# The scan's exponentiated rows: computed by ScalarE from rows already loaded, in place of stored once and loaded per chunk

## What is computed

```
a = -exp(log_a); dt = softplus(x @ Wdt.T + b_dt)
b, c = x @ Wb.T, x @ Wc.T                   # per head, state 64
state = exp(dt_t * a) * state + (dt_t * b_t) x_t      # step by step in time
y_t   = c_t . state
```

## Time and profile before

| | us |
|---|---|
| median of 3 runs | 1229.94 (1228.64 to 1230.48) |
| the profiled execution, its own time | 1230.54 |
| its span in the trace | 1228.7 |
| PE busy | 1208.2 (98%) |
| DVE, POOL, ACT busy | 949.7, 796.4, 611.8 |
| ecum_row loads | 128 of 128 KB, 3.7 to landing |

### The profile page before, as it was taken

One profiled execution on the slowest core, in us unless ns is written; L12 is line 12 of the kernel. 1 busy time (PEld: TensorE's weight loads), 2 busy tenths in 40 slices (PEclk: granted clock), 3 DMA queues, 4 the chain that ended last, 5 costly groups with the idle time before them and its releaser, 6 DMA issues.

```text
span 1228.7 us, 31470 instructions
## 1 busy us (share of the span) xinstructions
PE 1208.2 (98%) x12207; PEld 1012.2 (82%) x12207; DVE 949.7 (77%) x2028; ACT 611.8 (50%) x1279; POOL 796.4 (65%) x790
## 2 busy tenths in 40 slices
PE   8999999999999999999999999999999999999998
PEld 4666678888888888888888788898999889899998
DVE  7999977889876777777778667987777765776676
ACT  6999984434444443354344335543333332555454
POOL 4889955555555676776776648476666655576664
PEclk9999999999999999999999999999999999999999
DMA  9799756554455445555455456565544446799994
GB/s 298 261 337 356 288 214 170 149 157 146 157 157 160 154 146 170 161 150 164 149 148 168 126 171 212 190 156 91 109 91 90 97 87 125 251 320 322 336 332 166
DMA packets 140404, 231.40 MB, mean 188 GB/s; under 512 B 24416, under 2 KB 83040, under 8 KB 135648
## 3 DMA queue, kind: packets, MB, share of 16 engines
q1 hardware_dynamic: 127104, 212.10, 52.6%
q0 software_dynamic: 12288, 17.05, 8.1%
q10 hardware_dynamic: 864, 0.24, 0.1%
HBM read 147.81 MB, written 81.53 MB: 187 GB/s over the span
## 4 chain that ended last, share of the span: by engine, by line
PE 85%; DVE 5%; ACT 3%; DMA 3%; issue 2%; SPq 1%; POOL 1%; ACTq 0%; POOLq 0%; DVEq 0%
PE ps L1446 27%; PE ps L1808 11%; PE ps L2067 9%; PE ps L2301 7%; PE ps L2280 7%; PE ps L1527 4%; PE ps L1494 3%; PE ps L1553 3%; PE ps L1516 3%; PE ps L1538 2%; PE ps L1567 2%; PE ps L695 1%; DMA x_dram<-x 1%; PE ps L1787 1%; ACT tap L503 1%
## 5 line engine op out<-in xcount | busy, mean ns | idle before, releaser
L1408 ACT ACTIVATE decay<-tap,ncum 128x128 f32<-128x128 f32 x344 | 105.5, 389 | 191.7 <-POOL tap L1315 191.7
L1993 POOL DMA_INDIRECT ffn_dram<-ob,idx x64 | 110.5, 1727 | 81.8 <-DVE ob L1912 67.8
L2029 ACT ACTIVATE mid<-ps,b_up 128x512 f32<-128x512 f32 x96 | 66.1, 689 | 152.9 <-PE ps L1808 149.6
L1322 POOL TENSOR_TENSOR x_lo<-x,x_hi 128x512 fp32r<-128x512 f32 x56 | 76.9, 1372 | 100.4 <-ACT x_hi L1392 98.6
L1179 DVE TENSOR_TENSOR x_dt<-ps,dt 128x512 f32<-128x512 f32 x64 | 44.2, 691 | 126.4 <-PE ps L1553 126.3
L1446 PE MATMUL ps<-x_hi,w_hi_b 128*128 128x512 f32 x240 | 100.0, 416 | 2.0 <-issue 1.9
L1446 PE MATMUL ps<-x_hi,w_hi_c 128*128 128x512 f32 x240 | 99.3, 414 | 0.0
L2156 POOL TENSOR_SCALAR yc<-yc,gn_scale,gn_shift 128x512 f32<-128x512 f32 x56 | 76.3, 1374 | 33.1 <-DMA yc<-y_dram 33.1
L1446 PE MATMUL ps<-x_lo,w_hi_b 128*128 128x512 f32 x240 | 95.1, 396 | 0.0
L1408 ACT ACTIVATE decay<-cum_row,ncum 128x128 f32<-128x128 f32 x168 | 51.5, 391 | 86.8 <-POOL cum_row L1315 86.8
L1446 PE MATMUL ps<-x_lo,w_hi_c 128*128 128x512 f32 x240 | 94.2, 392 | 0.0
(11 more groups left out here) (321 smaller groups left out, 3996.9 us busy)
## 6 DMA issues: line engine op xcount, KB each, us to landing
tap<-cum_dram SPq DMA_DIRECT2D x86, 256.0 KB, 3.6
x_dram<-x SPq DMA_DIRECT2D x16, 1024.0 KB, 5.8
ecum_row<-ecum_dram SPq DMA_DIRECT2D x128, 128.0 KB, 3.7
yc<-y_dram SPq DMA_DIRECT2D x16, 1024.0 KB, 6.7
y_dram<-yb SPq DMA_DIRECT2D x60, 256.0 KB, 2.9
x<-x_dram SPq DMA_DIRECT2D x52, 256.0 KB, 3.9
cum_row<-cum_dram SPq DMA_DIRECT2D x42, 256.0 KB, 3.4
rows_dram<-xn SPq DMA_DIRECT2D x16, 512.0 KB, 3.3
```

The lines of the kernel that those rows point to most:

```text
L1322: nc.gpsimd.tensor_tensor(low, raw, high, ALU.subtract).then_inc(x_lo_ready, 1)
L1408: n = nc.scalar.activation(decay[g % 2][:, h, :], cum_row[g % NR][:, row, :], ACT.Exp, bias=t.ncum[:, g, h:h + 1])
L1993: pool.indirect_dma_start(out=t.ffn_dram, out_offset=bass.IndirectOffsetOnAxis(ap=t.idx[:, e, h * HC + c:h * HC + c + 1], axis=0), in_=ob[ ...
```

## The change

The exponentiated rows no longer go through DRAM. In the front, ecum, its transposes, its copy and its store are gone. In the scan ScalarE computes them from the rows of cum that are loaded anyway: exp_rows(g) waits for the load of those rows and for the product that last read its buffer, and writes ecum_row with two exponentials of 64 partitions x 512. In ScalarE's order exp_rows(g + 2) stands between b_part and c_part of chunk g (exp_rows(1) right after the first b_part). Since the mask overwrites the rows in place, causal(g) now waits for exp_rows(g) (ecum_ready). Chunks 0 and 32, which start with no state, have neither exp_rows nor c_dec. SyncE's 128 load_ecum are gone; the waits in front of the other transfers stay what they were, counted without the two chunks.

```diff
@@ front, VectorE
-            for i, bank in enumerate((ps_c, ps_dt)):
-                dve.wait_ge(ten, 3 + i)
-                do(v.tensor_copy(rowsT[:, i, :, :], bank[:, 0:GT * P].rearrange("p (g c) -> p g c", g=GT)),
-                   f"rows{i}")
+            dve.wait_ge(ten, 3)
+            do(v.tensor_copy(rowsT, ps_c[:, 0:GT * P].rearrange("p (g c) -> p g c", g=GT)), "rows")
@@ front, ScalarE
-            act.wait_ge(vec, steps["cum"])
-            nc.scalar.activation(tile_parity(ecum)[:, 0], by_tile_pair(t.cum[:, :, :])[:, 0], ACT.Exp)
-            nc.scalar.activation(tile_parity(ecum)[:, 1], by_tile_pair(t.cum[:, :, :])[:, 1], ACT.Exp).then_inc(sca, 1)
@@ scan, SyncE
-        def load_ecum(g):
-            until(sp, c_dec_ready, g - 1)
-            for a in range(2):
-                sp.dma_start(ecum_row[g % 2][a * HD:(a + 1) * HD, :, :],
-                             t.ecum_dram[g].rearrange("(a m) c -> a m c", a=2)[a].partition_broadcast(HD)
-                             ).then_inc(ecum_loaded[g % 2], 16)
...
                 load_cum(g + NR - 1, 0)
-                sp.wait_ge(c_dec_ready, g + 1)
+                until(sp, c_dec_ready, updates(g))
                 load_cum(g + NR - 1, 1)
...
-            if g + 2 < NT:
-                if g < LAST and not last:
-                    sp.wait_ge(s_mm, updates(g) + 1)
-                load_ecum(g + 2)
@@ scan, GpSimd: causal(g), decay_c(g) and the loop
             pool.wait_ge(cum_loaded[g % NR], 2 * loads(g, NR))
+            until(pool, ecum_ready, updates(g))
...
-            pool.wait_ge(ecum_loaded[g % 2], 2 * loads(g, 2))
+            pool.wait_ge(ecum_ready, updates(g))
...
-            decay_c(g)
+            if g % SPAN:
+                decay_c(g)
@@ scan, ScalarE
+        def exp_rows(g):
+
+            act.wait_ge(cum_loaded[g % NR], 2 * loads(g, NR))
+            until(act, c_dec_ready, updates(g - 2))
+            rows = cum_row[g % NR][:, :, :].rearrange("p (k a i) c -> p k a i c", k=2, a=2)
+            for a in range(2):
+                half = slice(a * HD, (a + 1) * HD)
+                n = nc.scalar.activation(ecum_row[g % 2][half, :, :].rearrange("p (k i) c -> p k (i c)", k=2),
+                                         rows[half, :, a].rearrange("p k i c -> p k (i c)"), ACT.Exp)
+            n.then_inc(ecum_ready, 1)
...
             if g == 0:
                 b_part(b + 1, c)
+                exp_rows(1)
...
             if b + 1 < NB:
                 if g:
                     b_part(b + 1, c)
+            if g + 2 < NT and (g + 2) % SPAN:
+                exp_rows(g + 2)
+            if b + 1 < NB:
                 c_part(b + 1, c)
@@ scan, TensorE
-                pe.wait_ge(c_dec_ready, g + 1)
+                pe.wait_ge(c_dec_ready, updates(g))
```

More of the change, by code:

```diff
@@ L160, in phase_front @@
         spare = [ring[:, i // 2, (i % 2) * BLK:(i % 2 + 1) * BLK] for i in range(2 * NX)]
-        u, e1, w1, ln, q, rec, dta, gap, ecum, dec8, lsum, eg = (
-            a.rearrange("p (t e) -> p t e", e=8) for a in spare[0:12])
-        rowsT = ring[:, 7, :].rearrange("p (i g c) -> p i g c", i=2, g=GT)
+        u, e1, w1, ln, q, rec, dta, gap, dec8, lsum, eg = (
+            a.rearrange("p (t e) -> p t e", e=8) for a in spare[0:8] + spare[9:12])
+        rowsT = ring[:, 7, 0:GT * P].rearrange("p (g c) -> p g c", g=GT)
         gates_g = t.cT0[:, 3, :].rearrange("p (g q e) -> p g q e", g=GT, e=E)
@@ L446, in _ @@
                       name="ncum")
-            for i, bank in enumerate((ps_c, ps_dt)):
-                dve.wait_ge(ten, 3 + i)
-                do(v.tensor_copy(rowsT[:, i, :, :], bank[:, 0:GT * P].rearrange("p (g c) -> p g c", g=GT)),
-                   f"rows{i}")
-            dve.wait_ge(sca, 8)
+            dve.wait_ge(ten, 3)
+            do(v.tensor_copy(rowsT, ps_c[:, 0:GT * P].rearrange("p (g c) -> p g c", g=GT)), "rows")
+            dve.wait_ge(sca, 7)
             for a in range(2):
@@ L454, in _ @@
                 do(v.tensor_copy(t.dec[half, :, :], dec8[half, :, a * MT:(a + 1) * MT]))
-            dve.wait_ge(ten, 5)
+            dve.wait_ge(ten, 4)
             do(v.tensor_copy(t.gateT[:, :], ps_x[3][:, 0:SEG]), "gateT")
@@ L790, in _ @@
             tile(4, range(2, MT))
[L791 to L803, removed]
+            pe.wait_ge(vec, steps["cum"])
+            for g in range(GT):
+                mm = pe.transpose(ps_c[:, g * P:(g + 1) * P],
+                                  t.cum[:, g * s.NSEG:(g + 1) * s.NSEG, :].rearrange("p t h -> p (t h)"), t.ident)
+            mm.then_inc(ten, 1)
+            tile(5)
+            pe.wait_ge(vec, steps["gates_g"])
+            for g in range(GT):
+                mm = pe.transpose(ps_x[3][:, g * P:(g + 1) * P],
+                                  gates_g[:, g, :, :].rearrange("p q e -> p (q e)"), t.ident)
+            mm.then_inc(ten, 1)
+            tile(6)
             tile(7)
@@ L934, in phase_scan @@
     cum_loaded = [sem(f"b_cum_loaded{i}") for i in range(NR)]
-    ecum_loaded = [sem(f"b_ecum_loaded{i}") for i in range(2)]
+    ecum_ready = sem("b_ecum")
     y_stored = [sem(f"b_y_stored{i}") for i in range(2)]
@@ L1212, in chunk @@
                     x.middle(dve, 0, f)
-        dve.wait_ge(t.front_sca, 8)
+        dve.wait_ge(t.front_sca, 7)
         begin()
@@ L1241, in load_x2 @@
             sp.dma_start(x2[b % NX][:, m, :], t.x2_dram[b, :, m, :]).then_inc(x2_loaded[b % NX], 16)
[L1243 to L1249, removed]
+        sp.wait_ge(t.front_vec, t.front_steps["rows"])
+        sp.dma_start(t.cum_dram.rearrange("(g t) h c -> (t h) g c", t=s.NSEG), t.rowsT).then_inc(t.cum_stored, 16)
+        sp.wait_ge(t.cum_stored, 16)
         for g in range(NR - 1):
@@ L1252, in _ @@
                 load_cum(g, k)
-        store_rows(1)
         sp.wait_ge(t.front_vec, t.front_steps["gateT"])
         sp.dma_start(x2[2][:, :, :], t.x2_dram[2]).then_inc(x2_loaded[2], 16)
-        sp.wait_ge(t.cum_stored[1], 16)
-        for g in range(2):
-            load_ecum(g)
         sp.wait_ge(zeroed, 1)
@@ L1325, in decay_c @@
             b, c = g // CH, g % CH
-            if g == 0:
+            if b == 0:
                 pool.wait_ge(t.tile_out, 2 * MT)
             until(pool, c_out, MT * b)
-            pool.wait_ge(ecum_loaded[g % 2], 2 * loads(g, 2))
+            pool.wait_ge(ecum_ready, updates(g))
             until(pool, y_mm, g)
-            until(pool, c_dec_ready, g)
+            until(pool, c_dec_ready, updates(g) - 1)
             nc.gpsimd.tensor_tensor(c_dec[:, :, :], cT[b % 2][:, :, c * P:(c + 1) * P], ecum_row[g % 2][:, :, :],
@@ L1542, in _ @@
         pe.wait_ge(t.tile_out, 2 * MT - 1)
-        pe.wait_ge(t.front_vec, t.front_steps["rows1"])
+        pe.wait_ge(t.front_vec, t.front_steps["rows"])
         for g in range(NT):
@@ L1694, in load_down @@
             sp.wait_ge(t.g_ready, CH * (s.NB - 1))
-            sp.wait_ge(t.c_dec_ready, CH * (s.NB - 1))
+            sp.wait_ge(t.c_dec_ready, t.updates(CH * (s.NB - 1) - 1))
         elif e == 1:
@@ L2385, in build @@
     t.cum_dram = dram("cum_dram", [s.NT, s.H, P])
-    t.ecum_dram = dram("ecum_dram", [s.NT, s.H, P])
     t.ffn_flat = t.ffn_dram.rearrange("(i p c) d -> i p (c d)", c=CH, p=P)
@@ L2428, in build @@
             t.parts_stored = sem("parts_stored")
-            t.x2_back, t.cum_stored = ([sem(f"{n}{i}") for i in range(2)] for n in ("x2_back", "cum_stored"))
-            t.x1_lo, t.tile_out, t.gates_stored = (sem(n) for n in ("x1_lo", "tile_out", "gates_stored"))
+            t.x2_back = [sem(f"x2_back{i}") for i in range(2)]
+            t.x1_lo, t.tile_out, t.gates_stored, t.cum_stored = (
+                sem(n) for n in ("x1_lo", "tile_out", "gates_stored", "cum_stored"))
             t.turned, t.load_turned = turned_pair, load_turned
```

## The result

The changed kernel takes 1249.43 us (median, 1247.59 to 1250.20), beside 1230.21 us (1228.64 to 1233.21) of the kernel before: a ratio of 1.0152, 95% interval 1.0136 to 1.0168, 19 us slower. Its profiled execution took 1247.59 us, with a span of 1245.7; before it was 1230.54 and 1228.7, so the traces explain 17.0 us, and the medians are 2 us further apart.

What follows compares the result with a forecast made beforehand. TensorE's own work was taken to set the pace (98% busy). Ends of blocks 17.2, start 1.0, end 0.6, less 2.4 for pauses, gave +16.4 on 1229.94: 1246.3 us; own range 1240 to 1250 (60 in 100), 8 in 10 for 1237 to 1258.

Steps and rivals of the forecast that it cites:

- Shares don't decide, the order does: Whole kernel: ScalarE is busy only 50%, yet cost depends on who waits for each changed instruction, and when.
- The time line of one end of a block: Chunk 55, T its start on TensorE: loads issued T + 3.87, seen T + 8.05, c_part T + 9.07, scores T + 9.73.
- Two exponentials, 1.02 us: ScalarE, 62 chunks: a pair of 64 x 512 delays what follows by 1.02 us; bounds 0.32 and 0.61 each.
- 14 x 1.2 + 0.4 = 17.2: Ends of blocks: TensorE waits 1.2 us for c_part at 14, 0.4 at chunk 31; 17.2 us, bounds 8.8 to 20.
- Issue pauses, half of chunk 15's and the whole of chunk 43's taken off, 2.4: Chunks 15 and 43: earlier "issue" pauses lie where TensorE will now stand anyway; 2.4 us off, bounds 0 and 9.8.
- Start 1.0: Chunk 1: the mask waits for exp_rows(1), so c_part reaches TensorE late; 1.0 us, bounds 0.5 and 1.5.
- End 0.6: Last block: exp_rows(63) delays GpSimd's last mask and c_dec(62), which TensorE needs; 0.6 us, bounds 0 and 2.
- Front and GpSimd at 0: Removed front work and two c_dec products are worth 0, as nobody waited; front bounds -0.4 and 0.
- Hidden: Ends of blocks: ScalarE has room and c_part isn't late, so time stays 1229 to 1231; 5 in 100.
- Relief of the transfers: Without the removed loads, 9.8 us of "issue" pauses go and rows land sooner: 1229.0, 4 in 100; half, 1239, 12.
- The clock: TensorE's clock falls in the new pauses: every third 8 us more, 1255; all 1270; 12 in 100 together.
- Stalls that feed themselves: Chunks 24 to 55: a late landing delays the next chunk through mask and decays; +8, 1255; 7 in 100.

Runs made afterwards that it cites:

- the first experiment: The changed kernel with one edit: c_part stands ahead of exp_rows in ScalarE's order; 1229.55 us, 0.9971 of the kernel before.
- the copy-first kernel: The changed kernel with c_part ahead of exp_rows in ScalarE's order; 1229.55 us (0.9971 of the kernel before), run once more 1227.40 us (0.9975).
- the third experiment: Each exponential pair made twice, once into an unread buffer: changed kernel with c_part ahead of exp_rows 1270.56 us (1.0304), changed kernel as is 1327.3 us (1.0764).

## Why the prediction was right, and where it was off

The forecast was 1246.3 us, the measurement 1249.43, inside the range and inside the likeliest case's own 1240 to 1250.

- *Shares don't decide, the order does*: right, and shown by the first experiment, in which the same work costs nothing.
- *The time line of one end of a block*: T + 3.87 for the issue, right; seen at T + 8.05, in chunk 55 T + 7.84; c_part at T + 9.07, measured T + 9.14; scores at T + 9.73, measured T + 9.83.
- *Two exponentials, 1.02 us*: this term was mis-sized. The pair delays the copy by 1.30 us, above my upper bound of 0.61 each. I took the pitch of two activations over all 128 partitions, where the second starts 0.10 us before the first ends. The two halves of 64 partitions don't overlap like that: 0.63 us each, and the copy 0.03 behind the second. 0.28 x 14 = 3.9 us, the sum's error at the ends of blocks: 9 plain ends gave 1.45 each, not 1.2.
- *14 x 1.2 + 0.4 = 17.2*: the ends grew by 21.3. Besides the pair: chunk 3 took 2.3, because its second load waited for a late c_dec (0.8 of it went with that wait), 59 took 2.1, and 31 1.75 in place of 0.4. In chunk 31 the exponentials start at T + 7.27 (500.24), where I had their rows landed at T + 6.3; that is 0.9 of the error, and the pair's 0.28 comes to it.
- *Issue pauses, half of chunk 15's and the whole of chunk 43's taken off, 2.4*: right. The two ends grew by 1.04 and 1.44 less than the plain ones, 2.5 us. But chunks 53 and 30 gave 5.9 more, which I had only in the bound (chunks 29, 41 and 49 took 1.4 of it back, chunks 2 and 18 gave 0.6). So the term, for the four places that I named, was 8.4 where I had 2.4. The stalls themselves, with these 2.5 added back, cost 23.8 where I had 17.2: 6.6 too little on one side and 6.0 on the other, and the total looks better than its parts.
- *Start 1.0*: chunks 0 and 1 took 1.7 more, above my bound of 1.5. Both waits that I named are there, the small product's on the state (0.98) and the projection's on the copy (0.36), one behind the other and not inside the same microsecond.
- *End 0.6*: the wait on c_dec came (0.9, no such wait stands before), but the chunks 60 to 62 together didn't grow (-0.2), as TensorE starts chunk 60 later than before against the other engines. In the copy-first kernel, where chunk 59 has no stall, they take 19.2 in place of 18.1: there the term shows, and is 1.1.
- *Front and GpSimd at 0*: chunk 0 starts 0.5 us sooner, a little beyond the bound of -0.4. In the copy-first kernel, with the same front, it starts 0.4 later than before (190.66, 190.74), so this is no gain that can be told from the scatter of the traces.

The rivals. *Hidden*: no; at no end of a block were the rows seen before T + 7.8, but for chunk 31 (T + 7.27). *Relief of the transfers*: a part of the half that I gave 12 in 100 happened beside the stalls, not its time of 1239: the stalls stayed, and the pauses of chunks 53 and 30 shrank by 5.9 us. Those of chunks 15 and 43 only lay beneath the stalls; in the copy-first kernel they are there again (10.8 and 10.4 to 10.7 us). What I held against it, that the other 60 fetches came in time, says nothing of these few. The Trainium skill (DMA: Bandwidth & Descriptors, Queues, rings and completion order) says that a DMA engine takes turns between its queues packet by packet, and I had concluded from it that relief would be small; the loads put back cost 0.3% (1.0003 against 0.9971, some 4 us), so the conclusion fails here, while no row shows a fetch's own wait and tests the rule itself. *The clock*: not in after, 1.00 behind pauses up to 2.1 us. But it was near: in the changed kernel without the wait on c_dec, chunk 59 ends in a pause of 2.13 us, and chunk 60 behind it has a clock of 0.72 (first two rows below). It is larger further out: in the changed order with pairs made twice, a pause of 4.09 us went with a clock of 0.72 (last two rows, columns as above), and the scores behind it took 1.56 us in place of 0.90:

```profile
776.85 0.90 PE L1485 MATMUL ps<-cT,bT 64*64 64x128 f32 x32 [2.13 <-issue]
777.68:783.78 6.10, 6.10 (x118) 5.68 (x112) 4.36 (x10) 5.16 (x13) 6.05 (x5) 0.72 0.54 125
...
538.00:550.00 12.00, 7.91 (x104) 6.38 (x103) 4.37 (x11) 7.78 (x19) 6.54 (x8) 0.72 0.20 57
544.10 1.56 PE L1494 MATMUL ps<-cT,bT 64*64 64x128 f32 x32 [4.09 <-issue]
```

*Stalls that feed themselves*: not in after: each of the chunks 4, 8, ..., 56, right behind an end of a block, is within 0.03 us of its length before, so nothing is handed on. But the path that I named, the mask behind ScalarE, is the closed loop of the third experiment, only 1.0 to 1.3 us away. I had named it and not added it up. Had I summed its legs against the chunk, 8 us against 9.3, its distance would have stood in the prediction, with what another microsecond costs.

## What to carry to other kernels

Work moved to an idle engine costs what stands behind it in that engine's order, so ask for each step with a wait which copy or release is queued behind it, and put that one first; here this alone turned 1.5% slower into 0.3% faster. Where a change makes one engine wait for another, look for the ring it closes (here load, exponentials, mask, product, next load), sum its legs, and hold the sum against the period of the loop: well below it the work is nearly free, above it each excess is paid again and again. And a good total can hide two errors that cancel; compare the terms one by one.

## What the hardware showed that I had not expected

- ScalarE's work over 64 partitions is as long as over 128: 0.63 us for 64 x 512 as for 128 x 512 (both in these runs). Two halves in a row took 1.27 to 1.30 us until the next instruction started, one whole 0.54.
- TensorE's pauses at "issue" stand in much the same chunks in kernels of different order. 256 KB of unread loads for each chunk cost 0.3% of the kernel's time; that they lengthen just these pauses is not shown.
- A pause of 2.09 us in chunk 3 of after left the clock at 1.00, one of 1.89 in the kernel before went with 0.88, and one of 2.13 in the changed kernel without the wait with 0.72 in the next chunk. So the length of a pause alone doesn't tell here whether the clock falls.
- The list of waits put 21.0 us down to "issue" of which the timeline shows 20.7 as one engine's copy. A label that names nobody is a reason to look at who ended just before.
